# Attention: the transposes of the row maxima stand after the fourth pair of key blocks instead of the fifth, ahead of its value products

## What is computed

```python
# first attention, 4 sequences of 512 rows, 16 heads of 16 columns
scores = einsum('bqhd,bkhd->bhqk', q, k) * scale
scores = where(tril, scores, -inf)
out = einsum('bhqk,bkhd->bqhd', softmax(scores), v).reshape(b, n, d)
x = layernorm(x + out @ Wo)
# second attention: the same form, all 16 heads share one k and one v
x = layernorm(x + ctx @ c_proj_w.T + c_proj_b)
```

## Time and profile before

| | us |
|---|---|
| median of three runs | 1139.42 |
| lowest and highest | 1137.05, 1142.79 |
| profiled execution | 1140.21 |
| its span | 1138.2 |
| TensorE busy in the span | 982.7 (86%) |
| VectorE busy | 633.5 (56%) |
| ScalarE busy | 484.5 (43%) |

### The profile page before, as it was taken

One profiled execution on the slowest core, in us unless ns is written; L12 is line 12 of the kernel. 1 busy time (PEld: TensorE's weight loads), 2 busy tenths in 40 slices (PEclk: granted clock), 3 DMA queues, 4 the chain that ended last, 5 costly groups with the idle time before them and its releaser, 6 DMA issues. The chain is left out here.

```text
span 1138.2 us, 22605 instructions
## 1 busy us (share of the span) xinstructions
PE 982.7 (86%) x8611; PEld 592.4 (52%) x8611; DVE 633.5 (56%) x2084; ACT 484.5 (43%) x1061; POOL 246.9 (22%) x496
## 2 busy tenths in 40 slices
PE   6865725888499999989998899898999998989997
PEld 3544724666345555448884455444555554844442
DVE  1874792333167777625335345404777772837765
ACT  2554502444225656633226864532656564620000
POOL 1661112455313333310003000000333334100000
PEclk9986558555569999979879998596999999989998
DMA  5045543122400720020000000000000001000000
GB/s 113 11 101 118 188 103 95 40 61 73 96 1 1 206 57 1 1 84 1 1 20 6 0 1 1 1 0 1 2 1 1 2 1 51 26 1 19 19 14 23
DMA packets 48691, 43.97 MB, mean 39 GB/s; under 512 B 8940, under 2 KB 41928, under 8 KB 48328
## 3 DMA queue, kind: packets, MB, share of 16 engines
q1 hardware_dynamic: 41976, 36.75, 12.4%
q10 hardware_dynamic: 6128, 4.21, 1.8%
q0 software_dynamic: 480, 1.57, 0.4%
HBM read 23.51 MB, written 14.81 MB: 34 GB/s over the span
## 5 line engine op out<-in xcount | busy, mean ns | idle before, releaser
L819 DVE CUSTOM_DVE_ANT_0 l_masked_scores<-psum,mask_q_rows 128x384 bf16<-128x384 f32 (+3 forms) x512 | 225.3, 488 | 75.3 <-PE psum L766 73.7
L841 ACT ACTIVATE l_probs<-psum 128x512 f32<-128x512 f32 (+1 forms) x384 | 181.5, 524 | 163.3 <-PE psum L752 161.7
L854 POOL TENSOR_SCALAR_AFFINE_SELECT l_probs<-l_probs 128x256 f32<-128x256 f32 x256 | 101.0, 407 | 397.0 <-ACT l_probs L841 396.8
L766 PE MATMUL psum<-kb_heads,q_heads 32*128 32x384 f32 (+3 forms) x512 | 113.1, 505 | 17.1 <-DVE l_neg_max_rows L808 15.5
L766 PE MATMUL psum<-l_k_heads,l_q_heads 32*128 32x384 f32 (+3 forms) x512 | 113.9, 507 | 4.2 <-DVE l_neg_max_rows L808 2.7
L752 PE MATMUL psum<-l_q_and_max,kb_heads 32*128 32x256 f32 (+3 forms) x512 | 114.8, 484 | 3.0 <-DVE l_q_and_max L825 2.8
L2086 PE MATMUL psum<-expert_w,rows_32k 128*128 128x512 f32 x256 | 116.0, 607 | 1.2 <-PEq L44 1.2
L752 PE MATMUL psum<-l_q_and_max,l_k_heads 32*128 32x256 f32 (+3 forms) x512 | 111.9, 473 | 3.0 <-DVE l_q_and_max L825 2.9
L784 PE MATMUL psum<-l_probs,rows_32k 128*32 128x512 f32 (+3 forms) x1024 | 99.9, 469 | 2.9 <-POOL l_probs L854 2.9
L752 PEld LDWEIGHTS psum<-l_q_and_max,kb_heads 32*128 32x128 f32 x512 | 58.4, 193 | 60.9 <-ACT l_probs L841 35.0
L752 PEld LDWEIGHTS psum<-l_q_and_max,l_k_heads 32*128 32x128 f32 x512 | 57.2, 187 | 58.5 <-ACT l_probs L841 32.9
(11 more groups left out here) (317 smaller groups left out, 1614.3 us busy)
## 6 DMA issues: line engine op xcount, KB each, us to landing
gram_scratch<-rows_32k SPq DMA_DIRECT2D x4, 1024.0 KB, 5.1
rows_32k<-v_new_and_ones SPq DMA_DIRECT2D x64, 64.0 KB, 2.0
x_rows<-in_L_attn_x_dram SPq DMA_DIRECT2D x16, 128.0 KB, 7.2
heads_scratch<-rows_32k SPq DMA_DIRECT2D x2, 1024.0 KB, 5.4
heads_scratch<-q_kb_T SPq DMA_DIRECT2D x2, 1024.0 KB, 6.0
inverse_scratch<-block_inv SPq DMA_DIRECT2D x2, 1024.0 KB, 4.1
q_heads<-heads_scratch SPq DMA_DIRECT2D x2, 1024.0 KB, 7.0
ent_w<-in_L_ffn_ent_w_dram SPq DMA_DIRECT2D x2, 1024.0 KB
```

Of the source, the lines that this page charges most:

```text
L766: mm = nc.tensor.matmul(ps[:, row_bank(G, u, i), o:o + w], QT(b, gq)[r, t * P:(t + 1) * P], KT(b, gq)[r, 0:w], start=True, stop=True)
L819: last = nc.vector.tensor_tensor_reduce(out=junk[:, ROW_AT[G, u] % 2, i, o:o + w], in0=ps[:, row_bank(G, u, i), o:o + w], in1=g.maskq[:, N ...
L841: nc.scalar.activation(PT[:, G % 2, 2 * (u % 2) + i, o:o + w], ps[:, e_bank(G, u, i), 0:w], ACT.Exp, scale=SCALE).then_inc(x_ok, 1)
L854: last = nc.gpsimd.affine_select(out=d, in_=d, pattern=[[0, 2], [1, P]], compare_op=ALU.is_ge, fill=0.0, base=0, channel_multiplier=-1)
```

## The change

The transposes move from behind the value products of the fifth pair to the place behind the fourth pair's matmuls, ahead of its value products. `ROW_ORDER` moves with them: the transposes' entry stands ahead of unit 1 of the group after, no longer behind it.

```diff
@@ ROW_ORDER
     for _k in range(UNITS):
         ROW_ORDER += row_units(_G, _k)
-        if _k == 4 and 0 <= _G + 1 < NGRP:
+        if _k == 3 and 0 <= _G + 1 < NGRP:
             ROW_ORDER.append((_G + 1, UNITS))
@@ phase_attention, TensorE
+                    if k == 3 and 0 <= G + 1 < NGRP:
+                        maxT(G + 1)
                     for kb, o in PV_AT.get(k, []):
                         if G >= 1:
                             pv(G - 1, kb, o)
-                    if k == 4 and 0 <= G + 1 < NGRP:
-                        maxT(G + 1)
```

## The result

| | before | after |
|---|---|---|
| median of 20 runs each, us | 1138.74 | 1131.74 |
| profiled execution's span, us | 1138.2 | 1132.3 |

The changed kernel is faster: ratio of the medians of undisturbed runs 0.994, 95% interval 0.9916 to 0.9965. One execution of it took 4600 us and is left out as disturbed. The forecast was 1133.5 us with a range of 1130 to 1139.

A forecast was written before the change was run, and what follows sets the result against it. TensorE was taken to bound the kernel, with waits inside its queue. Gains of 2.9 us per attention, 5.8 to 6 for both, took 1140.2 to 1134.3; the median's 0.8 lower gave 1133.5 us, range 1130 to 1139.

The forecast's parts named there:

- Step 1: Transposes behind the fourth pair: VectorE's reductions they need end in time, so no wait, 0.15 us to spare.
- Step 2: Fifth pair's row scores wait 0.33 us for VectorE's reductions; pair takes 0.65 from release, net cost about 0.11.
- Steps 3 and 4: Sixth pair to next group: add ready, 0.65 us, TensorE gains 0.18 a group; ScalarE lets 0.10 to 0.18 through.
- step 4: ScalarE behind the sixth pair: instructions overlap by 0.1 us, so 0.10 to 0.18 gets through; 0.18 taken.
- Step 5: VectorE: fifth pair's rows are reduced by 409.82, needed by the next group's first pair at 409.93; holds by 0.06 us.
- The sum: Each attention: 13 group changes x 0.18 = 2.3 us, last group 0.4, first about 0.2; both 5.8 to 6.
- The slower case: Fifth pair always needs 1.22 us from its release, next group 0.40 late: 1149 us; chance 0.10.
- The fifth pair as long as now: Fifth pair needs 0.82 to 0.88 us from release, group gains 0.01 or loses 0.05: 1138 to 1140; chance 0.04.
- ScalarE is bound: Rival: copy and following exponential can't overlap, leaving 0.00 to 0.10 us a group: 1136 to 1139; chance 0.12.
- The clock rival: A 3 us shift changes a last group's clock: 4.5 us gained (1129) or lost (1138); chance 0.05 each way.
- What would show it: Profile signs: `q_and_max` waits gone, about 14 fifth-pair waits of 0.3 us per attention, groups 9.92 apart, ScalarE idle 0.00 to 0.05.

The follow-up runs named there:

- early copy: Changed kernel with ScalarE's copy of the finished group ahead of the sixth pair's exponentials: groups 9.725 us apart; ratio 0.984 in one timing, not settled in another.
- k4 order: Kernel before with the transposes ahead of the fifth pair's value products instead of behind them: groups 9.89 us apart, 1128.63 us, ratio 0.992.

## Why the prediction came out

The time was 1131.7 us for 1133.5, a gain of 7.0 against 5.9. The mechanism is as written; the sizes of some terms are not. That the whole time came so near is in part luck: the same kernel gained 13.5 us in its second timing. What speaks for the mechanism is the distance of the groups, 9.90 for 9.92, and there a larger gain on TensorE and a loss behind it partly cancel.

- *Step 1, the transposes' own wait.* Right. They start at 403.67 behind the fourth pair without idle time, and it makes no difference whether the value products stand ahead of them or behind (9.90 both).
- *Step 2, the new wait.* Right in size: 0.34 for 0.33 (it reads 0.33 or 0.34 by kernel), the pair 0.64 from the release for 0.65, the net cost 0.10 for 0.11. The wait alone in the old order, and its absence in the new one, showed the two parts apart. The four matmuls of this pair take 0.64 to 0.65 in three kernels. The 0.82 estimated from the Trainium skill, "TensorE: Matmul & The Clock Gate", Part 3: Packing small matmuls, is not what they take here (that speedup is stated there for 512 columns), and the sixth pair of the trace was the better guide.
- *Steps 3 and 4.* The sixth pair goes from start to next group in 0.54, where I had put 0.65 from the fifth pair's way of letting the next start. One difference stands in the rows: the fifth pair is followed by value products on 128 rows, the sixth by a matmul on 32 rows. Whether that is the reason no run tests. With 0.54 the add cost the kernel before 0.40 a group (0.94 from 409.17 to 410.11), and not the 0.20 of the row or the 0.24 of the prediction. (That 0.24 has a slip too: 409.54 plus 0.30 is 409.84 and not 409.87, so 0.27 by starts; nothing else hangs on it.) From the fifth pair's start to the next group's, TensorE now needs 1.87 and the 0.58 of transposes that went ahead, 2.45 instead of 2.76 (407.35 to 410.11 in the earlier trace rows): 0.31 less, which is to 0.01 the 0.40 less the 0.10 of step 2. The group is only 0.20 shorter, so 0.11 is given back in the rest of it. That is ScalarE, as the early copy showed: the exponential starts 0.46 behind the copy's start (407.43 to 407.89), without idle time. I had 0.10 to 0.18 for what ScalarE lets through, and it was 0.20. The Trainium skill, "ScalarE: Activation LUTs", What ACT_TABLE_LOAD costs, says that back-to-back ACTIVATEs overlap by about 93 ns; the two exponentials of step 4 agree with 0.10, and from the copy to an exponential it is 0.13 (a copy of 0.59, the next start 0.46 behind its own).
- *Step 5.* VectorE holds less well than I had it. The slack of 0.06 is gone, since the next group starts 0.54 and not 0.65 behind the sixth pair: its first row scores wait for unit 1's reductions, 0.09 behind the first score matmul in every steady group. The group's second head waits for an exponential until 407.32 anyway, as step 5 says, so a cost of it is not seen; no run takes it away.
- *The sum.* 26 changes of group give 5.33 instead of 4.7. The first groups give 0.7 and 0.3 where I had 0.2, and the last ones 0.4 in the second attention for 0.4; in the first attention the stretch stayed at -0.1. The clock fits that: in the changed kernel's execution it was down to 0.50 from 478 us on, ahead of the last group's value products of 512 columns (they start at 479.14); before, these started at 483.60 and the clock was 0.98 over 480 to 484. The step up to these products takes 10.10 in this execution and 9.54 in the second profile of the same kernel, at full clock. Together 6.9 instead of 5.8 to 6.
- *The rivals.* The slower case is out: in a steady group the pair takes 0.64 from its release, and not 1.22. The fifth pair as long as now is out. ScalarE is bound, but at 0.20 a group and not at 0 to 0.10: the overlap was the point to settle, and the changed kernel's row of 407.89 settles it. The clock rival was right that the last group can take either clock, but it put this down to a shift by the change, and the same kernel shows both. Its price was too low: I had read 4.5 us from one stretch, and the same kernel's first attention differs by 7.4 between two executions with the one and the other clock in its last group.
- *What would show it.* One sign failed: about 14 listed waits of L766 for L819. The wait is there, at every fifth pair, but the four that are listed, with 1.1 us in all, are the first group's. The row names idle time of the engine, and the first head's score matmul covers nearly all of it. It is seen from the starts alone, 404.82 and 405.16, and from the release at 405.10.

## What to carry to other kernels

When an instruction moves in a queue, price the pair behind each wait from its release and not from its start: a pair that waited for something else at the same time (here an exponential) gets that back. A wait that left the list is not shown to be gone: lay the start beside the end of what it waited for, and see whether their distance is that of a known release (0.15 behind the add, before and in the k4 order). Then ask which engine has less slack than the gain, since it takes what is left; it can be read from the idle time in one row ahead (0.20 here). And measure a change of 0.5% by a distance that repeats within the profile, such as that of neighbouring groups, beside the whole time.

## What was not expected of the hardware

- A wait inside TensorE's queue does not show as idle time when the instruction ahead of it is still busy: the list of waits names none of the steady groups for what the starts show as 0.34 in each, and none for the add in the k4 order, where every group starts 0.15 behind the add's end.
- VectorE's add starts with the last accumulator read and not behind it (both at 413.86 in one kernel, both at 405.02 in the other), as a following reduction does (both at 407.53 in the kernel before).
- The last group of the first attention ran at 1.2 GHz in one execution of a kernel and at 2.4 in another, with all the groups before at equal distances; the attention is 7.4 us longer in the first. That is more than the change itself gives.
